# Queries, keys and values of two images as 64-row matmuls side by side, and values moved from unit 1 to unit 3

## The chip, the cores and the metric

The kernel runs on one core of a Trainium2 chip. The metric is the device time of that core in microseconds. Three runs of the kernel before gave 184.57, 183.47 and 184.43 us, a median of 184.43 us.

## The reference, cut to what matters

The input is 32 images of 64 channels by 16 x 16 pixels. A gate comes first, then group norm and attention with 4 heads of 16 channels over the 256 pixels of each image.

```
def _L0_conv_ref(x, w_c, w_s):               # channel gate, then spatial gate
    y = conv1d(mean(x, (2, 3)), w_c); yc = sigmoid(x * y)
    sa = sigmoid(conv2d(concat(mean(yc, 1), max(yc, 1)), w_s))
    return yc * sa + x

def _L1_conv_ref(x, gn_w, gn_b, qkv_w, qkv_b, proj_w, proj_b):
    xn = groupnorm(x, 32 groups) * gn_w + gn_b
    q, k, v = split(einsum('bchw,oc->bohw', xn, qkv_w) + qkv_b, 3)
    attn = softmax(einsum('bndi,bndj->bnij', q, k) / sqrt(16))
    out = einsum('bnij,bndj->bndi', attn, v)
    return x + einsum('bchw,oc->bohw', out, proj_w) + proj_b
```

## The kernel before

Two images make a pair: image 0 of a pair lies on partitions 0 to 63, image 1 on partitions 64 to 127, one channel each. There are 16 pairs. The attention is a software pipeline: `pipeline(eng, turn)` (L186) runs `turn(k)` on every engine for k = -5 to 17, and one turn holds eight units u = 0 to 7, one for each image and head. The order inside a turn is written out by hand, the same on each engine, and engines meet only at semaphores. In turn k, TensorE works on several pairs at once:

- `s(u)` (L761, matmuls L768) makes the scores of pair k+1 for unit u: two bf16 matmuls of 256 columns. VectorE takes their maximum over a row (L608). Two banks alternate, so `s(u)` waits for the maximum of unit u-2.
- `st(u)` (L772, matmuls L780) makes the transposed scores with the maximum subtracted by one extra row; ScalarE turns them into exponentials (L448).
- `maxt()` (L841, matmul L847) at unit 0 transposes the maxima of pair k. It waits for the last maximum of the turn before, and for `gn_var` of that turn, which VectorE writes after it (L561).
- `qk(a, d)` (L798, matmul L805) makes queries and keys of image a into its half of `z_bank`: all 128 partitions of `xn` against a weight matrix whose rows for the other image are zero. The call is float32, and the trace shows each float32 matmul as two MATMUL instructions. Image 0 of pair k+4 comes at unit 7 of turn k, image 1 of the same pair at unit 0 of the turn after. ScalarE reads the bank twice, at unit 0 (L456) and unit 1 (L459, `z32`), and GpSimd and SyncE split it into bf16 parts and spread them through DRAM.
- `v()` (L809, matmul L815) at unit 1 makes the values of both images of pair k+1, pixels by channels: per 128 pixels one float32 matmul with `xn` as weights and a block-diagonal 128 x 128 `w_v` as moving operand. ScalarE copies them to `vs` at unit 2 (L465).
- `pv(a)` (L784, matmul L794) at units 2 and 4 multiplies exponentials and values of pair k-1 in float32, with weights of 32 columns, four heads on four column groups. `proj()` (L818, matmul L824) at unit 4 does the output projection of pair k-2, also with weights of 32 columns.
- `groupstats(5)` (L828) at unit 6 serves the group norm of pair k+5, and GpSimd (L339 to L365) and ScalarE (L440, `xn`) finish it.
- VectorE also transposes and normalises the output of `pv`: L575, L579, L581, L586.

In PSUM, banks 0 to 3 belong to `s` and `st`, bank 4 to `pv`, bank 5 to `z_bank`, bank 6 to `v_psum`, `mt_psum` and `gs_psum`, bank 7 to `y_psum` of `proj`.

Of the kernel before, what the change touches and what calls it, by code (L numbers as in the profile page):

```python
# [38 lines left out]
MAPS = ((0, 1), (1, 2)) + tuple((p, p + 2) for p in range(2, PAIRS, 2))  # L39
EPS = 1e-5  # L40
LEAD = HEADS
SCALE = float(HD) ** -0.5
TWIN = (SIDE // TILES + KS - 1) * SIDE
HALO = KS // 2 * SIDE
# [10 lines left out]
def program(nc, x, vecs, w_all, select, consts, out):  # L55
    ctx = ExitStack()
    with ctx:
# [3 lines left out]
        def sem(name):  # L61
            return ctx.enter_context(nc.semaphore(name))

        quad = ctx.enter_context(nc.psum_tensor("quad", [P, 4, 512], F32))
        bank = [quad[:, i, :] for i in range(4)] + [ctx.enter_context(nc.psum_tensor(f"bank{i}", [P, 512], F32)) for i in range(4, 8)]
        parts_dram = nc.dram_tensor("parts_dram", [RING, 3, 2, HD, HEADS * 2 * N], BF16).ap()
        gate_dram = nc.dram_tensor("gate_dram", [IMAGES, N], F32).ap()

# [35 lines left out]
        negmax = sb("negmax", [P, RING, P], BF16)  # L104
        maxrow = sb("maxrow", [16, RING, P], BF16)
        pt = sb("pt", [P, UNITS, TILES, N])
        vs = sb("vs", [P, RING, TILES, 2, HEADS, 2 * HD])
        rstd = sb("rstd", [P, 1])
        mhalf = sb("mhalf", [P, 1])
        eps = sb("eps", [P, 1])  # L110
# [14 lines left out]
        st_bank = [bank[2], bank[3]]  # L125
        o_bank = bank[4]
        z_bank = bank[5]
        v_psum = bank[6][:, 0:256]
        mt_psum = bank[6][:, 320:384].bitcast(BF16)
        y_psum = bank[7][:, 0:256]  # L130
        gs_psum = bank[6][:, 400:403]


# [47 lines left out]
        def stands_in(aside, k, u):  # L181

            if isinstance(k, int) and (k, u) in aside:
                aside[k, u]()

        def pipeline(eng, turn):  # L186

# [121 lines left out]
        @block.gpsimd  # L309
        def _(pool):  # L310
            nc.gpsimd.memset(eps[:, :], EPS).then_inc(eps_ready, 1)
            nc.gpsimd.memset(mhalf[:, :], -0.5).then_inc(mhalf_ready, 1)
            nc.gpsimd.memset(warm[:, :], 0.0).then_inc(warm_ready, 1)
            nc.gpsimd.memset(negmax[:, :, :], 0.0).then_inc(negmax_zero, 1)
            pool.wait_ge(mhalf_ready, 1)
            pool.wait_ge(eps_ready, 1)

            nc.gpsimd.memset(vs[:, :, :, :, :, :].rearrange("p r t a h d -> p (r t a h) d")[:, :, HD:2 * HD], 1.0).then_inc(fixed_ready, 1)
            pool.wait_ge(fixed_ready, 1)
            nc.gpsimd.memset(ks[KQ:KQ + 1, :, :, :, :], 1.0).then_inc(fixed_ready, 1)  # L320
            pool.wait_ge(fixed_ready, 2)
            pool.wait_ge(vec_in, 16)

            def turn(k, slot, has, lap):

                if has(-3):
                    wait(pool, yo_ready, k - 2)
                    nc.gpsimd.tensor_tensor(at(xall, k - 3), yo[:, slot(-3), :], at(xall, k - 3), ALU.add).then_inc(out_ready, 1)  # L328

                if has(5) and not (isinstance(k, int) and k + 5 in EARLY):  # L330
                    if isinstance(k, int) and k + 4 in EARLY:
                        pool.wait_ge(x1_ready, k + 5)
                    for g in [(k + 5) // GROUP] if isinstance(k, int) else range(1, GROUPS):
                        pool.wait_ge(gate_in[g], 32)
                    nc.gpsimd.tensor_tensor(at(ycall, k + 5), at(ycall, k + 5), at(gate, k + 5), ALU.mult).then_inc(u_ready, 1)  # L335
                    pool.wait_ge(u_ready, k + 6)
                    nc.gpsimd.tensor_tensor(at(xall, k + 5), at(ycall, k + 5), at(xall, k + 5), ALU.add).then_inc(x1_ready, 1)

                if has(4):  # L339
                    wait(pool, gn_var, k + 5)  # L340
                    nc.gpsimd.tensor_tensor(sq[:, :], gmv[:, 2:3], gmv[:, 2:3], ALU.mult).then_inc(sq_ready, 1)  # L341
                    nc.gpsimd.tensor_tensor(posvar[:, :], eps[:, :], gmv[:, 1:2], ALU.subtract).then_inc(posvar_ready, 1)
                    wait(pool, sq_ready, k + 5)
                    wait(pool, posvar_ready, k + 5)
                    nc.gpsimd.tensor_tensor(vareps[:, :], sq[:, :], posvar[:, :], ALU.add).then_inc(vareps_ready, 1)
                    wait(pool, vareps_ready, k + 5)
                    nc.gpsimd.tensor_tensor(rstd[:, :], vareps[:, :], mhalf[:, :], ALU.pow).then_inc(rstd_ready, 1)

                on_pool = has(3) and not (isinstance(k, int) and k + 3 == 0)
                if on_pool:  # L350
                    r = slot(3)
                    wait(pool, p1_ready, k + 4)
                    wait(pool, z32_ready, k + 3)
                    wait(pool, split_step, 3 * (k + 3))
                    nc.gpsimd.tensor_tensor(rest[:, :], z32[:, :], parts[:, r, 0, :], ALU.subtract).then_inc(split_step, 1)  # L355
                    wait(pool, split_step, 3 * (k + 3) + 1)

                if has(4):
                    wait(pool, rstd_ready, k + 5)
                    wait(pool, xn_ready, k + 4)  # L360
                    nc.gpsimd.tensor_tensor(gna[:, :], rstd[:, :], w_gn, ALU.mult).then_inc(gn_scale, 1)
                    wait(pool, gn_scale, k + 5)
                    nc.gpsimd.tensor_tensor(gnm[:, :], gmv[:, 0:1], gna[:, :], ALU.mult).then_inc(gn_mean, 1)
                    wait(pool, gn_mean, k + 5)
                    nc.gpsimd.tensor_tensor(gnb[:, :], gnm[:, :], b_gn, ALU.add).then_inc(gn_shift, 1)  # L365
                if on_pool:
                    nc.gpsimd.tensor_scalar(parts[:, r, 1, :], rest[:, :], 1.0, 0.0, ALU.mult, ALU.add).then_inc(split_step, 1)
                    wait(pool, st_ready, UNITS * k)
                    wait(pool, split_step, 3 * (k + 3) + 2)
                    nc.gpsimd.tensor_tensor(parts[:, r, 2, :], rest[:, :], parts[:, r, 1, :], ALU.subtract).then_inc(split_step, 1)  # L370
            pipeline(pool, turn)
# [3 lines left out]
        def _(act):  # L375
# [54 lines left out]
            def turn(k, slot, has, lap):  # L430
                for u in range(UNITS):
# [19 lines left out]
                    if u == 0 and has(3):  # L451
                        wait(act, z_ready, k + 4)
                        wait(act, parts_out[0], 16 * (k - 1))
                        if isinstance(k, int) and k == 1:
                            act.wait_ge(stack_in[0], 2 * SLOTS * 16)
                        nc.scalar.activation(parts[:, slot(3), 0, :], z_bank[:, :], ACT.Identity, bias=b_qk).then_inc(p1_ready, 1)  # L456
                    if u == 1 and has(3) and not (isinstance(k, int) and k + 3 == 0):
                        wait(act, split_step, 3 * (k + 2) + 1)
                        nc.scalar.activation(z32[:, :], z_bank[:, :], ACT.Identity, bias=b_qk).then_inc(z32_ready, 1)  # L459

                    if u == 2 and has(1):
                        if isinstance(k, int) and k == -1:
                            act.wait_ge(pbias_ready, 1)
                        wait(act, v_ready, k + 2)
                        nc.scalar.copy(vs[:, slot(1), :, :, :, :].rearrange("p t a h d -> p (t a h) d")[:, :, 0:HD],  # L465
                                       v_psum.rearrange("p (g d) -> p g d", d=HD)).then_inc(vs_ready, 1)

                    if u == 5 and has(-2) and not (isinstance(k, int) and k - 2 == PAIRS - 1):
                        wait(act, y_ready, k - 1)
# [166 lines left out]
        def _(pe):  # L636
# [123 lines left out]
            def turn(k, slot, has, lap):  # L760
# [23 lines left out]
                def pv(a):  # L784
# [6 lines left out]
                        wait(pe, vs_ready, k)  # L791
                    for t in range(TILES):
                        for h in range(HEADS):
                            mm = pe.matmul(o_bank[32 * h:32 * h + 32, a * N:(a + 1) * N], vs[:, slot(-1), t, a, h, :],  # L794
                                           pt[:, HEADS * a + h, t, :], start=(t == 0), stop=(t == TILES - 1))
                    mm.then_inc(pv_done, 1)

                def qk(a, d):  # L798
# [7 lines left out]
                    if a == 1:  # L806
                        mm.then_inc(z_ready, 1)

                def v():  # L809

                    wait(pe, mrow_ready, k + 1)
                    if has(4):
                        wait(pe, gn_var, 4 if isinstance(k, int) and k == 0 else k + 5)
                    for t in range(TILES):
                        mm = pe.matmul(v_psum[:, t * P:(t + 1) * P], xn[:, slot(1), t * P:(t + 1) * P], w_v, start=True, stop=True)  # L815
                    mm.then_inc(v_ready, 1)

                def proj():  # L818

                    wait(pe, norm_step, 4 * PAIRS + 4 if isinstance(k, int) and k == PAIRS + 1 else 4 * (k - 1))  # L820
                    wait(pe, yo_ready, k - 2)
                    for a in range(2):
                        for j in range(0, C, 32):
                            mm = pe.matmul(y_psum[C * a + j:C * a + j + 32, :], w_p[:, j:j + 32], onorm[:, a * N:(a + 1) * N],  # L824
# [26 lines left out]
                for u in range(UNITS):  # L851
# [9 lines left out]
                    if u == 0 and has(0):  # L861
                        maxt()
                    if u == 0 and has(3) and not first_turns:
                        qk(1, 3)
                    if u == 1 and has(1):
                        v()
                    if u == 2 and has(-1):
                        pv(0)
                    if u == 4 and has(-2):
# [4 lines left out]
                        groupstats(5)  # L874
                    if u == 2 and isinstance(k, int) and k == 0:
                        groupstats(4)
                    if u == 7 and has(4) and not (first_turns and k < -1):
                        qk(0, 4)
                    if first_turns:
                        beginning(k, u, qk, groupstats)  # L880
# [59 lines left out]
```

## Time and profile before

| what | value |
|---|---|
| median of 3 runs | 184.43 us |
| profiled execution, its own time | 184.61 us |
| its span, first to last instruction | 182.6 us |
| mean granted TensorE clock | 0.947 |
| TensorE matmul busy | 163.2 us |
| VectorE busy | 136.5 us |
| ScalarE busy | 121.6 us |
| GpSimd busy | 106.3 us |

The busy time of TensorE counts overlapping matmuls once, and the ends of its matmuls are modelled; the start of one matmul to the start of the next is the firmer measure. Outside the span lie 2.0 us of the profiled execution's own time.

### The profile page before, as it was taken

The numbers are of one execution on the slowest core, as the hardware profiler recorded it, in microseconds if no ns is written. First come the engines' busy times: TensorE is split into PE (matmuls) and PEld (weight loads), VectorE is DVE, ScalarE is ACT, GpSimd is POOL, SyncE is SP. The second block draws the span as 40 slices with busy tenths as digits, with TensorE's granted clock in tenths as the row PEclk, the third lists the DMA queues.
The fourth block names the chain that finished last, engine by engine and source line by source line (L and its number), as shares of the span: only waits on it lengthen the run. The fifth ranks groups of instructions, "written<-read, shape, count | busy, mean of one in ns | idle before, by whom it ended". The sixth has DMA issues, their size and how long they took to land.

```text
span 182.6 us, 4762 instructions
## 1 busy us (share of the span) xinstructions
PE 163.2 (89%) x1508; PEld 107.3 (59%) x1511; DVE 136.5 (75%) x280; ACT 121.6 (67%) x254; POOL 106.3 (58%) x206
## 2 busy tenths in 40 slices
PE   6988829999685999999999999999999999998791
PEld 3778428776451857666675766767575754553220
DVE  1567663677661889898998989899897978876433
ACT  3552343455682679887987988798797965758730
POOL 8926072681977267888888778888858350101110
PEclk9999955899997899999999999999999999999967
DMA  5940487516189544555464564564646465110001
GB/s 138 336 149 0 100 105 224 153 59 176 63 196 232 151 134 130 173 164 187 130 204 148 162 201 148 169 183 163 173 132 186 139 203 148 36 32 30 29 0 57
DMA packets 19296, 25.31 MB, mean 139 GB/s; under 512 B 3568, under 2 KB 16400, under 8 KB 19280
## 3 DMA queue, kind: packets, MB, share of 16 engines
q1 hardware_dynamic: 18560, 24.62, 46.2%
q10 hardware_dynamic: 720, 0.48, 1.6%
q8 instruction: 9, 0.15, 0.4%
q14 instruction: 7, 0.06, 0.1%
HBM read 16.22 MB, written 8.02 MB: 133 GB/s over the span
## 4 chain that ended last, share of the span: by engine, by line
PE 77%; DVE 5%; ACT 4%; POOL 4%; issue 3%; DMA 2%; ACTq 2%; SPq 2%; POOLq 0%
PE bank L794 17%; PE quad L768 16%; PE quad L780 14%; PE bank L805 7%; PE bank L824 5%; PE quad L662 5%; PE bank L815 4%; PE bank L640 2%; DMA qs<-maxrow 2%; PE bank L674 2%; ACT pt L448 2%; ACTq L217 2%; DVE negmax L608 2%; PE bank L838 1%; POOL rest L355 1%
## 5 line engine op out<-in xcount | busy, mean ns | idle before, releaser
L608 DVE TENSOR_REDUCE negmax<-quad 128x2 bf16<-128x512 f32 x128 | 83.4, 678 | 21.1 <-PE quad L768 19.4
L448 ACT ACTIVATE pt<-quad 128x512 f32<-128x512 f32 x128 | 72.8, 594 | 23.2 <-PE quad L780 23.2
L780 PE MATMUL quad<-qs,ks 97*128 97x256 bf16 x256 | 49.4, 275 | 6.7 <-ACT pt L448 3.5
L768 PE MATMUL quad<-ks,qs 96*128 96x256 bf16 x256 | 50.5, 279 | 1.2 <-DVE negmax L608 0.4
L794 PE MATMUL bank<-pt,vs 128*32 128x256 f32 x512 | 35.8, 399 | 0.0
L768 PEld LDWEIGHTS quad<-ks,qs 96*128 96x128 bf16 x256 | 21.9, 101 | 22.3 <-DVE negmax L608 13.1
L780 PEld LDWEIGHTS quad<-qs,ks 97*128 97x128 bf16 x256 | 23.8, 98 | 14.7 <-ACT pt L448 6.3
L328 POOL TENSOR_TENSOR xall<-yo,xall 128x256 f32 (+1 forms) x15 | 11.0, 731 | 31.7 <-ACT yo L472 31.7
L794 PEld LDWEIGHTS bank<-pt,vs 128*32 128x32 f32 x512 | 15.1, 112 | 12.9 <-ACT pt L448 3.3
L355 POOL TENSOR_TENSOR rest<-z,parts 128x512 f32<-128x512 f32 x15 | 17.3, 1156 | 8.0 <-issue 5.9
L805 PE MATMUL bank<-xn,wall 128*128 128x256 f32 x64 | 19.9, 397 | 0.0
L370 POOL TENSOR_TENSOR parts<-rest,parts 128x512 bf16<-128x512 f32 x15 | 17.3, 1155 | 1.5
L456 ACT ACTIVATE parts<-bank,vec 128x512 bf16<-128x512 f32 x16 | 10.8, 675 | 10.4 <-PE bank L805 7.3
L575 DVE STREAM_TRANSPOSE otok<-bank 128x512 f32<-128x512 f32 (+1 forms) x17 | 11.5, 677 | 5.9 <-PE bank L794 5.9
L440 ACT ACTIVATE xn<-xall,gnb,gna 128x256 f32<-128x256 f32 (+1 forms) x16 | 9.6, 599 | 7.4 <-POOL gnb L365 7.2
L341 POOL TENSOR_TENSOR sq<-gmv 128x1 f32<-128x1 f32 x16 | 3.1, 194 | 17.5 <-DVE gmv L561 17.4
L586 DVE STREAM_TRANSPOSE onorm<-otok 128x512 f32<-128x512 f32 (+1 forms) x17 | 11.6, 680 | 1.2 <-PE bank L824 0.6
L824 PE MATMUL bank<-onorm,wall 128*32 128x256 f32 x128 | 10.7, 406 | 1.6 <-DVE onorm L586 1.6
L662 PE MATMUL quad<-con,ycall 128*128 128x130 f32 x64 | 10.8, 321 | 0.1
L805 PEld LDWEIGHTS bank<-xn,wall 128*128 128x128 f32 x64 | 10.0, 194 | 1.1 <-issue 0.6
L335 POOL TENSOR_TENSOR ycall<-ycall,gate (+1 forms) x12 | 8.7, 726 | 3.3 <-DMA gate<-gate_dram 3.3
L815 PE MATMUL bank<-wall,xn 128*128 128x128 f32 x64 | 10.4, 287 | 0.0
(66 smaller groups left out, 207.7 us busy)
## 6 DMA issues: line engine op xcount, KB each, us to landing
parts_dram<-parts SPq DMA_DIRECT2D x45, 128.0 KB, 2.0
ks<-parts_dram SPq DMA_DIRECT2D x15, 192.0 KB, 3.0
qs<-parts_dram SPq DMA_DIRECT2D x15, 192.0 KB, 3.2
out<-xall SPq DMA_DIRECT2D x16, 128.0 KB, 2.1
qs<-parts_dram SPq DMA_DIRECT2D x15, 128.0 KB, 2.7
ks<-parts_dram SPq DMA_DIRECT2D x15, 128.0 KB, 2.8
xall<-x SPq DMA_DIRECT2D x3, 512.0 KB, 6.0
gate<-gate_dram SPq DMA_DIRECT2D x6, 256.0 KB, 4.1
```

Source lines behind the costliest of these rows:

```text
L355: nc.gpsimd.tensor_tensor(rest[:, :], z32[:, :], parts[:, r, 0, :], ALU.subtract).then_inc(split_step, 1)
L370: nc.gpsimd.tensor_tensor(parts[:, r, 2, :], rest[:, :], parts[:, r, 1, :], ALU.subtract).then_inc(split_step, 1)
L448: nc.scalar.activation(pt[:, (u + LEAD) % UNITS, :, :].rearrange("p t n -> p (t n)"), st_bank[u % 2][:, :], ACT.Exp, scale=SCALE).then_inc ...
L586: op = nc.vector.transpose(onorm[:, cols], o_tok[:, blocks, :].rearrange("p b c -> p (b c)"))
L608: nc.vector.tensor_reduce(negmax[:, slot(1), column:column + TILES], s_bank[u % 2][:, :].rearrange("p (t n) -> p t n", t=TILES), AX.X, ALU ...
L662: mm = pe.matmul(bank[MAP_BANK[i] + p - first][:, t * (P + 2):(t + 1) * (P + 2)], ycall[:, p, t * P:(t + 1) * P], con[:, C_IDENT:C_TOEP], ...
L768: mm = pe.matmul(s_bank[u % 2][:, t * N:(t + 1) * N], qs[0:KQ, slot(1), h, a, t * P:(t + 1) * P], ks[0:KQ, slot(1), h, a, :], start=True, ...
L780: mm = pe.matmul(st_bank[u % 2][:, t * N:(t + 1) * N], ks[0:KQ + 1, slot(d), h, a, t * P:(t + 1) * P], qs[0:KQ + 1, slot(d), h, a, :], sta ...
L794: mm = pe.matmul(o_bank[32 * h:32 * h + 32, a * N:(a + 1) * N], vs[:, slot(-1), t, a, h, :], pt[:, HEADS * a + h, t, :], start=(t == 0), s ...
L805: mm = pe.matmul(z_bank[:, a * N:(a + 1) * N], w_qk[a], xn[:, slot(d), :], start=True, stop=True)
L815: mm = pe.matmul(v_psum[:, t * P:(t + 1) * P], xn[:, slot(1), t * P:(t + 1) * P], w_v, start=True, stop=True)
L824: mm = pe.matmul(y_psum[C * a + j:C * a + j + 32, :], w_p[:, j:j + 32], onorm[:, a * N:(a + 1) * N], start=True, stop=True)
```

## The change

Three things change. (1) From turn 1 on (`apart(k)`), `qk_apart` replaces the two calls of `qk`: at unit 0 it makes queries and keys of both images of pair k+3, each with the 64 rows of its own image as contraction, into different banks; nothing of it is left at unit 7. (2) From turn 1 on, `v_apart` replaces `v`: four float32 matmuls of 64 rows by 128 weight columns and 64 moving columns, image 0 to one bank and image 1 to another, at unit 3 in place of unit 1; ScalarE's copy goes from unit 2 to unit 3. (3) PSUM is laid out as one tensor of eight banks so that `z_halves` and `v_halves` straddle two neighbouring banks; `y_psum` moves to the bank of `z`, `vs` has image before tile, and waits are added for what now shares a bank.

```diff
+FIRST_APART = 1
-        quad = ctx.enter_context(nc.psum_tensor("quad", [P, 4, 512], F32))
-        bank = [quad[:, i, :] for i in range(4)] + [ctx.enter_context(nc.psum_tensor(f"bank{i}", [P, 512], F32)) for i in range(4, 8)]
+        quad = ctx.enter_context(nc.psum_tensor("quad", [P, 8, 512], F32))
+        bank = [quad[:, i, :] for i in (0, 1, 2, 3, 4, 5, 7, 6)]
-        vs = sb("vs", [P, RING, TILES, 2, HEADS, 2 * HD])
+        vs = sb("vs", [P, RING, 2, TILES, HEADS, 2 * HD])
+        z_halves = quad[:, 5:7, :].rearrange("p b (h n) -> p (b h) n", n=N)[:, 1:3, :]
+        v_halves = quad[:, 6:8, :].rearrange("p b n -> p (b n)")[:, 384:640]
-        y_psum = bank[7][:, 0:256]
+        y_psum = bank[5][:, 0:256]
+        def apart(k):
+            return not isinstance(k, int) or k >= FIRST_APART
...
-                        nc.scalar.activation(parts[:, slot(3), 0, :], z_bank[:, :], ACT.Identity, bias=b_qk).then_inc(p1_ready, 1)
+                        nc.scalar.activation(per_image(parts[:, slot(3), 0, :]), queries_of(k), ACT.Identity, bias=b_qk).then_inc(p1_ready, 1)
...
-                    if u == 2 and has(1):
+                    if u == (3 if apart(k) else 2) and has(1):
...
+                def qk_apart():
+
+                    wait(pe, xn_ready, k + 4)
+                    wait(pe, z32_ready, k + 2)
+                    wait(pe, yo_ready, k - 2)
+                    for a in range(2):
+                        mm = pe.matmul(z_halves[:, a, :], w_qk[a][C * a:C * (a + 1), :], xn[C * a:C * (a + 1), slot(3), :], start=True, stop=True)
+                    mm.then_inc(z_ready, 1)
...
+                def v_apart():
+
+                    wait(pe, mrow_ready, k + 1)
+                    if has(4):
+                        wait(pe, gn_var, k + 5)
+                    if has(3):
+                        wait(pe, z32_ready, k + 3)
+                    for t in range(TILES):
+                        for a in range(2):
+                            at_ = (a * TILES + t) * C
+                            mm = pe.matmul(v_halves[:, at_:at_ + C], xn[C * a:C * (a + 1), slot(1), t * P:(t + 1) * P],
+                                           w_v[C * a:C * (a + 1), C * a:C * (a + 1)], start=True, stop=True)
+                    mm.then_inc(v_ready, 1)
...
                     wait(pe, yo_ready, k - 2)
+                    if has(3):
+                        wait(pe, z32_ready, k + 3)
...
                     if u == 0 and has(3) and not first_turns:
-                        qk(1, 3)
-                    if u == 1 and has(1):
+                        if apart(k):
+                            qk_apart()
+                        else:
+                            qk(1, 3)
+                    if u == 1 and has(1) and not apart(k):
                         v()
+                    if u == 3 and has(1) and apart(k):
+                        v_apart()
...
-                    if u == 7 and has(4) and not (first_turns and k < -1):
+                    if u == 7 and has(4) and not apart(k + 1) and not (first_turns and k < -1):
                         qk(0, 4)
```

## Rows read from the trace of the kernel before

**Rows 1.** Chain that ended last: start us, us, what; 11 repeats from first to last.
```profile
61.77 0.43 PE bank L805 x2
...
141.28 0.43 PE bank L805 x2
```

**Rows 2.** Busy time by stretch: window, length, busy us (instructions) of each engine, clock.
```profile
core 0: us, PE busy (x) PEld busy (x) DVE busy (x) ACT busy (x) POOL busy (x), PEclk, DMA share, GB/s
88.36:96.32 7.96, 7.96 (x90) 5.49 (x91) 7.38 (x16) 6.79 (x16) 6.63 (x14) 1.00 0.56 169
```

**Rows 3.** Timeline of TensorE matmuls in one turn: start us, us, what.
```profile
89.55 0.38 PE L780 MATMUL quad<-qs,ks 97*128 97x256 bf16 x2
...
90.00 0.38 PE L780 MATMUL quad<-qs,ks 97*128 97x256 bf16 x2
90.31 0.64 PE L824 MATMUL bank<-onorm,wall 128*32 128x256 f32 x8
90.76 1.05 PE L794 MATMUL bank<-pt,vs 128*32 128x256 f32 x16
91.74 0.39 PE L768 MATMUL quad<-ks,qs 96*128 96x256 bf16 x2
...
93.44 0.59 PE L805 MATMUL bank<-xn,wall 128*128 128x256 f32 x2
93.87 0.38 PE L768 MATMUL quad<-ks,qs 96*128 96x256 bf16 x2
94.09 0.38 PE L780 MATMUL quad<-qs,ks 97*128 97x256 bf16 x2
94.32 0.22 PE L847 MATMUL bank<-identb,negmax 128*128 128x128 bf16 x1
94.38 0.65 PE L805 MATMUL bank<-xn,wall 128*128 128x256 f32 x2
94.86 0.38 PE L768 MATMUL quad<-ks,qs 96*128 96x256 bf16 x2
...
95.30 0.61 PE L815 MATMUL bank<-wall,xn 128*128 128x128 f32 x4
95.75 0.38 PE L768 MATMUL quad<-ks,qs 96*128 96x256 bf16 x2
```

**Rows 4.** Timeline of VectorE, same turn; in brackets the idle time before.
```profile
92.17 1.93 DVE L608 TENSOR_REDUCE negmax<-quad 128x2 bf16<-128x512 f32 x3 [0.39 <-PE quad L768]
...
94.02 0.15 DVE L561 TENSOR_SCALAR gmv<-bank 128x3 f32<-128x3 f32 x1
```

**Rows 5.** Timeline of weight loads (PEld), same turn.
```profile
94.29 0.10 PEld L847 LDWEIGHTS bank<-identb,negmax 128*128 128x128 bf16 x1
...
95.20 0.52 PEld L815 LDWEIGHTS bank<-wall,xn 128*128 128x128 f32 x4
```

**Rows 6.** Timeline around the only matmuls with few rows (4).
```profile
20.16 1.13 PE L695 MATMUL quad<-gate_s,sel 4*128 4x256 f32 x4
21.22 0.70 PE L805 MATMUL bank<-xn,wall 128*128 128x256 f32 x2
```

**Rows 7.** Those matmuls by line: durations min/median/max ns, first and last start.
```profile
L695 PE MATMUL quad<-gate_s,sel x4: 374/374/478, 20.2 to 20.9; 4*128 4x256 f32 x4
```

**Rows 8.** Timeline of the first 0.08 us of a 16-matmul group.
```profile
88.32 0.42 PE L794 MATMUL bank<-pt,vs 128*32 128x256 f32 x4
```

**Rows 9.** Timeline of ScalarE in the same turn.
```profile
88.31 0.69 ACT L459 ACTIVATE z<-bank,vec 128x512 f32<-128x512 f32 x1
...
92.89 0.47 ACT L472 ACTIVATE yo<-bank,pbias 128x256 f32<-128x256 f32 x1
```

**Rows 10.** Timeline of TensorE in turns 1 and 13, with idle time before.
```profile
57.01 0.38 PE L780 MATMUL quad<-qs,ks 97*128 97x256 bf16 x2 [3.04 <-DMA qs<-maxrow]
...
153.74 0.38 PE L780 MATMUL quad<-qs,ks 97*128 97x256 bf16 x2 [0.42 <-ACT pt L448]
```

More of the change, by code:

```diff
@@ L184, in stands_in, with queries_of, per_image @@
                 aside[k, u]()
+        def apart(k):
+            return not isinstance(k, int) or k >= FIRST_APART
+        def queries_of(k):
+            return z_halves if apart(k) else per_image(z_bank[:, :])
+        def per_image(t):
+            return t.rearrange("p (a n) -> p a n", a=2)
         def pipeline(eng, turn):
@@ L316, in _ @@
             pool.wait_ge(eps_ready, 1)
-            nc.gpsimd.memset(vs[:, :, :, :, :, :].rearrange("p r t a h d -> p (r t a h) d")[:, :, HD:2 * HD], 1.0).then_inc(fixed_ready, 1)
+            nc.gpsimd.memset(vs[:, :, :, :, :, :].rearrange("p r a t h d -> p (r a t h) d")[:, :, HD:2 * HD], 1.0).then_inc(fixed_ready, 1)
             pool.wait_ge(fixed_ready, 1)
@@ L455, in turn @@
                             act.wait_ge(stack_in[0], 2 * SLOTS * 16)
-                        nc.scalar.activation(parts[:, slot(3), 0, :], z_bank[:, :], ACT.Identity, bias=b_qk).then_inc(p1_ready, 1)
+                        nc.scalar.activation(per_image(parts[:, slot(3), 0, :]), queries_of(k), ACT.Identity, bias=b_qk).then_inc(p1_ready, 1)
                     if u == 1 and has(3) and not (isinstance(k, int) and k + 3 == 0):
                         wait(act, split_step, 3 * (k + 2) + 1)
-                        nc.scalar.activation(z32[:, :], z_bank[:, :], ACT.Identity, bias=b_qk).then_inc(z32_ready, 1)
-                    if u == 2 and has(1):
+                        nc.scalar.activation(per_image(z32[:, :]), queries_of(k), ACT.Identity, bias=b_qk).then_inc(z32_ready, 1)
+                    if u == (3 if apart(k) else 2) and has(1):
                         if isinstance(k, int) and k == -1:
@@ L464, in turn @@
                         wait(act, v_ready, k + 2)
-                        nc.scalar.copy(vs[:, slot(1), :, :, :, :].rearrange("p t a h d -> p (t a h) d")[:, :, 0:HD],
-                                       v_psum.rearrange("p (g d) -> p g d", d=HD)).then_inc(vs_ready, 1)
+                        nc.scalar.copy(vs[:, slot(1), :, :, :, :].rearrange("p a t h d -> p (a t h) d")[:, :, 0:HD],
+                                       (v_halves if apart(k) else v_psum).rearrange("p (g d) -> p g d", d=HD)).then_inc(vs_ready, 1)
                     if u == 5 and has(-2) and not (isinstance(k, int) and k - 2 == PAIRS - 1):
@@ L793, in pv @@
                         for h in range(HEADS):
-                            mm = pe.matmul(o_bank[32 * h:32 * h + 32, a * N:(a + 1) * N], vs[:, slot(-1), t, a, h, :],
+                            mm = pe.matmul(o_bank[32 * h:32 * h + 32, a * N:(a + 1) * N], vs[:, slot(-1), a, t, h, :],
                                            pt[:, HEADS * a + h, t, :], start=(t == 0), stop=(t == TILES - 1))
@@ L814, in v @@
                     for t in range(TILES):
-                        mm = pe.matmul(v_psum[:, t * P:(t + 1) * P], xn[:, slot(1), t * P:(t + 1) * P], w_v, start=True, stop=True)
+                        mm = pe.matmul(v_psum.rearrange("p (a t n) -> p a t n", a=2, t=TILES)[:, :, t, :], xn[:, slot(1), t * P:(t + 1) * P], w_v,
+                                       start=True, stop=True)
+                    mm.then_inc(v_ready, 1)
[10 more added lines that the diff above has]
+                                           w_v[C * a:C * (a + 1), C * a:C * (a + 1)], start=True, stop=True)
                     mm.then_inc(v_ready, 1)
```

## The prediction

> **What bounds the kernel now.** I read the chain that ended last first. Between 60 and 142 us it runs almost only through TensorE, and its pieces repeat: the matmuls of `qk` for image 0 stand in it eleven times, from 61.77 to 141.28 us [rows 1]. That is 79.51 us for ten turns, a period of 7.95 us. Then I read the busy time of one such turn: TensorE 7.96 of 7.96 us, at the full clock (1.00, the 2.4 GHz level), VectorE 7.38 us, ScalarE 6.79 and GpSimd 6.63 [rows 2]. TensorE paces these turns, but VectorE is close behind. VectorE waits for scores once in a turn, 0.39 us before the maximum of unit 5 [rows 4], so a turn can't get shorter than 7.95 - 0.39 = 7.56 us whatever TensorE saves.
>
> Third, the timeline of a turn shows who waits for whom. `s(5)` starts at 91.74; the maximum of unit 5 starts 0.43 us later, three maxima take until 94.10, and `gmv` ends at 94.02 + 0.15 = 94.17 [rows 3, 4]. `maxt` waits for `gmv`, and its weight load starts at 94.29 [rows 5], 0.12 us later. Some 0.04 us of that goes to the semaphore (the maximum starts 0.04 us after the end of the matmul at 91.74 + 0.39), so 0.08 us is left. So there is a loop through both engines: `s(5)`, three maxima, `gmv`, `maxt`, and then all of TensorE's work down to the next `s(5)`. It takes 7.95 - 0.08 = 7.87 us now. It is this loop that decides: work taken from TensorE between `s(5)` and `maxt` saves 0.08 us at most, work added behind `maxt` counts in full.
>
> **Removed.** From start to start of the next matmul, `qk` of image 0 at unit 7 takes 93.87 - 93.44 = 0.43 us, `qk` of image 1 94.86 - 94.38 = 0.48 us, `v` 95.75 - 95.30 = 0.45 us [rows 3]. The first lies before `maxt`: of its 0.43 us the loop gets 0.08.
>
> **Price of changing the shape of the array.** The change puts 64-row matmuls between 128-row ones. The trace has no 64-row matmul, but has two kinds of neighbours. The first are `proj` and `pv`, of 32 weight columns. Into `proj`: the second matmul of `st(4)` starts 0.11 us (half of the 0.22 between rows) after 90.00 and takes 0.11, so it is through at 90.22, and `proj` starts at 90.31, 0.09 us late. Out of `pv(1)`: its 16 matmuls start at 90.76; at four column groups side by side they need 4 x 0.213 = 0.853 us (0.213 is half of `qk`'s 0.43); `s(5)` starts at 91.74, 0.13 us late [rows 3]. The second neighbour is the gate's pair of matmuls with 4 rows and 128 weight columns. Their first lasts 478 ns against 374 for the others, so 0.10 us of weight load is laid bare, and after the last start, 20.9 + 0.21 us, the next 128-row matmul starts 0.11 us late [rows 6, 7]. I take 0.09 + 0.10 in and 0.13 out, 0.32 us each visit, since the new weights too have 128 float32 columns. Bounds: nothing (it never shows) and 0.42 us, with another 0.10 us for a bare load on the way out, as 0.70 us for two `qk` matmuls there against 0.59 in the steady turn suggests [rows 3, 6].
>
> The Trainium skill speaks here (TensorEngine Tiling (Array Packing), Key Properties): changing the tiling mode, not merely the tile, drains the engine. By that rule the 64-row case is no exception to the rows just read; no run here shows that case yet.
>
> **Added at unit 0: `qk_apart`.** Two float32 matmuls of 256 columns on two halves of the rows, four instructions. If the halves run side by side, 2 x 0.213 = 0.43 us. That column groups do so shows in the four `pv` matmuls that start within 0.08 us [rows 8]; for row groups no row shows it, so the bounds are 0.43 and 0.85 us. I take 0.43, since the nearest row is a concurrent one. With the visit: 0.43 + 0.32 = 0.75 us. What it replaces behind `maxt` is 0.48 us plus nothing else. The difference is +0.27; a little of the load is already bare after `maxt` (0.48 against 0.43) and is counted in both.
>
> **Added at unit 3: `v_apart`.** Half the moving columns, but eight weight loads of 128 columns where there were four. The four loads of `v` take 0.52 us and one 0.19, so they come every (0.52 - 0.19)/3 = 0.11 us [rows 5], and `v` is already paced by loads as much as by columns. With the halves side by side: four loads, 0.10 (in the visit's price) + 3 x 0.11 + 0.05 for the last 64 columns = 0.38 us and the 0.32, 0.70 us. If the loads of the halves follow each other, four more: +0.43, 1.13 us. If only columns counted, 4 x 0.053 = 0.21. I take 0.70, by concurrency as above. Against 0.45 removed, +0.25 us. Its move from unit 1 to unit 3 keeps it in the same stretch between `maxt` and `s(5)`, so the move neither helps nor hurts the loop.
>
> By the same page's Theoretical Speedup, 64 rows give up to twofold. By that alone `qk_apart` would cost 0.43 and `v_apart` 0.22 us, and the loop would fall to VectorE's floor; that result is the first rival below.
>
> **Edits at nothing.** `v_apart` waits for `z32`, with `s(4)`, `st(4)`, `proj`, `pv(1)` queued behind it. `z32` is ready at 88.31 + 0.69 = 89.00 [rows 9], `st(3)` is through at 89.77 [rows 3]: 0.77 us of cover; without it each late bit would count in full. `proj`'s wait for `z32` has 1.3 us. `qk_apart` waits for `yo`, done at 93.36, 1 us before [rows 9]. ScalarE's copy of the values comes about 1.2 us later; the first who wait are `groupstats` at unit 6 and then `maxt`, both over a microsecond away. The ScalarE instructions that read two banks have the same elements (bound: 0.1 us each if they were slower, covered by 1.2 us of ScalarE's idle time). SyncE's and GpSimd's orders don't change; their input `z` comes at 94.24 + 0.05 + 0.19 + 0.43 and the same latency, within 0.1 us of now. Turn 1 waits 3.04 us for a DMA behind `v`'s new place [rows 10], so its edits are hidden. In turn 13 `st(4)` waits 0.42 us for ScalarE [rows 10], which covers the move of `v` there; turn 14 may add 0.25.
>
> **Sum.** The loop: 7.87 + 0.27 + 0.25 = 8.39 us, +0.44 us a turn. TensorE's own total is lower, 7.95 - 1.36 + 1.45 = 8.04 us, so it would idle some 0.35 us a turn before `maxt`. From `s(5)` of turn 1 to that of turn 12 are eleven turns: 11 x 0.44 = +4.8 us. Against the profiled execution's own 184.61 us that is 189.4 us; this execution lies 0.18 us above the median, so 189.2, and I say 189.0, a little of the visit's price being perhaps shared with the gap already behind `maxt`.
>
> **Rivals.**
> (a) *Visits cost nothing and loads hide, faster.* Next weights are fetched while the last 128-row matmuls run, and the halves overlap. The price from which it decides: below 0.06 us a visit (2 x 0.32 less 0.52) the loop is no longer than 7.87, and faster than now by over 1% needs also `v`'s loads to shrink. With `v_apart` at 0.21 and `qk_apart` at 0.43 the loop is 7.87 - 0.05 - 0.24 = 7.58 us, at VectorE's floor of 7.56: 11 x -0.37 = -4.1, 180.4 us. With loads at their pace, 7.87 - 0.05 - 0.02 = 7.80: -1.7, 182.8 us. For it: the halves touch different rows. Against it: the 4-row pair paid on both sides [rows 6, 7]. Chance 0.15.
> (b) *About half the visit's price*, because some of it is latency that the next row's start hides: 8.39 - 0.32 = 8.07, +0.12 a turn, 185.8 us. TensorE's own total then lies beneath the loop. Chance 0.15.
> (c) *Halves overlap as matmuls, but their weight loads come one after another*: +0.43 more in `v_apart`, loop 8.82, +0.87 x 11 = 9.6, 194.0 us. Chance 0.12.
> (d) *Row halves don't run side by side at all, the change does not do what it says*: +0.43 in `qk_apart` as well, loop 9.25, +14.3, 198.7 us. Chance 0.07.
>
> **How the numbers follow.** The forecast has 0.51. A measurement of this kernel tells about 1% (1.8 us) from no change. Faster by over 1%, below 182.6: 0.12, most of (a). Within 1%: 0.16, the rest of (a) and most of (b), whose 185.8 lies just inside. Slower: 0.72. The range leaves out what of (a) lies below its upper value (0.11) and (d) (0.07), with the least of the edges: 182.7 to 194.2. The forecast's own range is 187 to 191.
>
> **What would show it.** In a steady turn of the changed kernel: from the start of `qk_apart`'s first matmul to the next `s` about 0.6 to 0.7 us, with a gap ahead of it; from `v_apart`'s first start to `s(4)` about 0.6; the four instructions of `qk_apart` starting in twos shows the overlap, one by one shows (d). Eight loads of `v_apart` in about 0.5 us against 0.9 tells the forecast from (c). TensorE idle before `maxt`, ended by `gmv`, shows the loop, and VectorE's idle time before unit 5 should grow from 0.39 to about 0.8. A period under 7.95 us would make the prediction wrong, and so would 64-row matmuls whose loads start before the last 128-row matmul has ended.

## The result and the profile after

The changed kernel is slower. Six runs have a median of 192.56 us (189.46 to 193.26), against 184.12 us (182.69 to 185.91) for the kernel before; the ratio is 1.035, with a 95% interval of 1.028 to 1.043. The ratios and intervals, here and in the table below, compare only executions outside a slower state that both kernels fall into at times, so they aren't the quotients of the medians: of the changed kernel two of the six remain (190.30 and 189.46 us), and where the table says none, too few remain. The forecast of 189.0 us was 1.025 times the median then shown. The profiled execution took 192.36 us, its span is 190.4 us.

The chain that ended last in the changed kernel, where the 16 matmuls of `pv(1)` mark a turn (start us, us, what; turns 2, 12 and 15):

```profile
68.88 0.86 PE quad L806 x16
...
153.60 0.86 PE quad L806 x16
...
176.81 0.97 PE quad L806 x16
```

And the same three marks in the kernel before:

```profile
67.08 0.86 PE bank L794 x16
...
146.57 0.86 PE bank L794 x16
...
168.96 0.97 PE bank L794 x16
```

The 7.8 us between the two spans (190.4 - 182.6) divide so: 68.88 - 67.08 = 1.8 us up to turn 2; ten turns of 8.47 instead of 7.95 us, 84.72 - 79.49 = 5.2 us; three turns after them 23.21 instead of 22.39 us, 0.8 us; and the rest, 13.59 against 13.64, nothing. Half of the first piece comes before turn 1 (ScalarE's `maxrow` copy of turn 1 starts at 51.32 against 50.43 us), where the two kernels do the same work but for the layout of PSUM. It doesn't come with the change: the changed kernel profiled once more was at that copy at 49.37 us, and its whole span was 188.5 us. Of the other half, 0.40 us lies between that copy and `st(4)` of turn 1, which waits for the DMA of the maxima (6.98 us against 6.58; 6.79 in the second profile), so that part isn't shown to be the change's either. The remaining 0.51 us are the two visits of turn 2 to 64 rows. The change thus accounts for 0.5 + 5.2 + 0.8 = 6.5 us, which is 3.5% of 184 us.

One turn of the changed kernel, the timeline of TensorE (start us, us, what; it answers to [rows 3]):

```profile
92.24 0.38 PE L792 MATMUL quad<-qs,ks 97*128 97x256 bf16 x2
92.55 0.66 PE L850 MATMUL quad<-wall,xn 64*128 64x64 f32 x8
93.14 0.39 PE L780 MATMUL quad<-ks,qs 96*128 96x256 bf16 x2
...
93.69 0.64 PE L862 MATMUL quad<-onorm,wall 128*32 128x256 f32 x8
94.14 1.05 PE L806 MATMUL quad<-pt,vs 128*32 128x256 f32 x16
95.12 0.39 PE L780 MATMUL quad<-ks,qs 96*128 96x256 bf16 x2
...
97.27 0.39 PE L792 MATMUL quad<-qs,ks 97*128 97x256 bf16 x2
97.70 0.22 PE L885 MATMUL quad<-identb,negmax 128*128 128x128 bf16 x1
97.98 0.70 PE L827 MATMUL quad<-xn,wall 64*128 64x256 f32 x4
98.61 0.39 PE L780 MATMUL quad<-ks,qs 96*128 96x256 bf16 x2
```

`qk_apart` takes 98.61 - 97.98 = 0.63 us and `v_apart` 93.14 - 92.55 = 0.59 us from start to start, each with a gap ahead of it: `v_apart` starts 92.55 - 92.24 = 0.31 us after `st(3)`, where 0.22 is usual. `qk_apart` starts 0.28 us after `maxt` here and 0.14 in most turns, against 0.06 before (94.38 - 94.32 in [rows 3]). In the median over the steady turns these four distances add up to 0.14 + 0.64 + 0.31 + 0.59 = 1.68 us, and what they replace to 0.06 + 0.48 + 0.22 + 0.45 = 1.21 us. That is 0.47 of the 0.50 us by which a turn grew; all other distances between `maxt` and `s(5)` are those of before to 0.01 us, so the new layout of PSUM and the added waits cost nothing there. The weight loads of the same turn, with the idle time before them and what ended it:

```profile
92.55 0.52 PEld L850 LDWEIGHTS quad<-wall,xn 64*128 64x128 f32 x8 [0.21 <-issue]
...
97.67 0.10 PEld L885 LDWEIGHTS quad<-identb,negmax 128*128 128x128 bf16 x1 [0.29 <-DVE negmax L620]
97.95 0.33 PEld L827 LDWEIGHTS quad<-xn,wall 64*128 64x128 f32 x4 [0.18 <-issue]
98.61 0.11 PEld L780 LDWEIGHTS quad<-ks,qs 96*128 96x128 bf16 x2 [0.33 <-issue]
```

Eight loads of `v_apart` take 0.52 us, as four of `v` did [rows 5]: the two row halves load side by side. No load stands ahead of a change of shape; each begins within 0.03 us of its matmul, where `v`'s loads began 0.10 us ahead (95.20 against 95.30 in [rows 3, 5]). `maxt`'s load now waits idle for VectorE. VectorE in that turn (it answers to [rows 4]):

```profile
95.55 1.93 DVE L620 TENSOR_REDUCE negmax<-quad 128x2 bf16<-128x512 f32 x3 [0.82 <-PE quad L780]
97.40 0.15 DVE L573 TENSOR_SCALAR gmv<-quad 128x3 f32<-128x3 f32 x1
```

Its wait for the scores of unit 5 grew from 0.39 to 0.82 us, and the three maxima and `gmv` follow `s(5)` at the same distances as before. Busy times of one such turn (it answers to [rows 2]):

```profile
81.00:89.46 8.46, 8.43 (x92) 5.03 (x91) 7.33 (x16) 6.95 (x14) 6.63 (x14) 1.00 0.52 154
```

TensorE's busy time reads 8.43 of 8.46 us though it waits at `maxt` and at each change of shape: the modelled ends of its matmuls cover these gaps, and only starts show them. The granted clock is at its full level (1.00) in both kernels' steady turns. It isn't so around turn 1: there TensorE waits about 3 us for the DMA of the maxima (3.04 us before, 2.93 after), and right behind that wait the clock reads 0.50, the 1.2 GHz level, before the change in the window of 58 to 60 us, after it in that of 60 to 62 us.

### The profile page after: what moved, and what is told of

Read it like the earlier page. It is cut to its first block, busy times and chain, and to the rows that moved or that the text cites. A ratio compares the mean times of both kernels' runs of the same rounds, so it can differ in the third digit from the quotient of the medians.

```text
span 190.4 us, 4883 instructions
## 1 busy us (share of the span) xinstructions
PE 170.0 (89%) x1567; PEld 102.5 (54%) x1567; DVE 136.2 (72%) x280; ACT 123.9 (65%) x254; POOL 106.3 (56%) x206
## 3 DMA queue, kind: packets, MB, share of 16 engines
HBM read 16.22 MB, written 8.02 MB: 127 GB/s over the span
## 4 chain that ended last, share of the span: by engine, by line
PE 75%; DVE 8%; issue 4%; ACT 4%; POOL 4%; DMA 2%; ACTq 2%; SPq 1%; POOLq 0%
PE quad L780 16%; PE quad L806 16%; PE quad L792 13%; PE quad L862 5%; PE quad L674 5%; PE quad L850 4%; PE quad L827 4%; DVE negmax L620 3%; PE quad L652 3%; DMA qs<-maxrow 2%; PE quad L686 2%; ACTq L229 2%; PE quad L876 1%; PE quad L817 1%; ACT pt L460 1%
## 5 line engine op out<-in xcount | busy, mean ns | idle before, releaser
L460 ACT ACTIVATE pt<-quad 128x512 f32<-128x512 f32 x128 | 74.0, 596 | 28.8 <-PE quad L792 28.8
L806 PE MATMUL quad<-pt,vs 128*32 128x256 f32 x512 | 35.5, 397 | 0.0
L780 PEld LDWEIGHTS quad<-ks,qs 96*128 96x128 bf16 x256 | 18.9, 101 | 27.2 <-DVE negmax L620 15.9
L806 PEld LDWEIGHTS quad<-pt,vs 128*32 128x32 f32 x512 | 15.1, 112 | 12.7 <-issue 3.8
L468 ACT ACTIVATE parts<-quad,vec 128x512 bf16<-128x512 f32 x16 | 11.0, 685 | 11.7 <-PE quad L817 7.5
L587 DVE STREAM_TRANSPOSE otok<-quad 128x512 f32<-128x512 f32 (+1 forms) x17 | 11.5, 677 | 5.9 <-PE quad L806 5.9
L862 PE MATMUL quad<-onorm,wall 128*32 128x256 f32 x128 | 10.7, 406 | 1.6 <-DVE onorm L598 1.6
L471 ACT ACTIVATE z<-quad,vec 128x512 f32<-128x512 f32 x15 | 10.3, 687 | 0.0
L674 PEld LDWEIGHTS quad<-con,ycall 128*128 128x128 f32 x64 | 9.6, 226 | 0.8 <-issue 0.4
L652 PE MATMUL quad<-warm 128*128 128x512 bf16 x19 | 8.5, 494 | 1.4 <-POOL warm L325 1.4
```

Of the source, the lines that this page charges most:

```text
L460: nc.scalar.activation(pt[:, (u + LEAD) % UNITS, :, :].rearrange("p t n -> p (t n)"), st_bank[u % 2][:, :], ACT.Exp, scale=SCALE).then_inc ...
L587: op = nc.vector.transpose(o_tok[:, blocks, :].rearrange("p b c -> p (b c)"), o_bank[:, cols])
L652: pe.matmul(bank[:, :], warm[:, 0:P], warm[:, :], start=True, stop=True)
L674: mm = pe.matmul(bank[MAP_BANK[i] + p - first][:, t * (P + 2):(t + 1) * (P + 2)], ycall[:, p, t * P:(t + 1) * P], con[:, C_IDENT:C_TOEP], ...
L780: mm = pe.matmul(s_bank[u % 2][:, t * N:(t + 1) * N], qs[0:KQ, slot(1), h, a, t * P:(t + 1) * P], ks[0:KQ, slot(1), h, a, :], start=True, ...
```

## The experiments

The totals of these kernels spread by some microseconds from run to run, and the profiles show much of it ahead of the steady turns: ScalarE's `maxrow` copy of turn 3 starts anywhere from 70.3 to 76.6 us, at 72.44 and at 70.32 us in two profiles of the changed kernel. So the steady turn is read from each trace: the distance between the starts of ScalarE's `maxrow` copies, once a turn, the median and the mean of the eight turns from turn 3 to turn 11.

| kernel | median turn | mean turn | ratio to before (95%) |
|---|---|---|---|
| before | 7.96 | 7.96 | 1 |
| changed | 8.46 | 8.51 | 1.035 (1.028 to 1.043) |
| values only | 8.34 | 8.35 | 1.011 (0.994 to 1.029) |
| queries and keys only | 8.21 | 8.25 | none |
| values only moved, 128 rows | 8.10 | 8.17 | 1.006 (0.997 to 1.015) |
| queries and keys at unit 7 | 7.94 | 7.99 | 1.012 (0.999 to 1.026) |
| before with a 64-row visit | 8.38 | 8.38 | none |
| before with its 128-row twin | 8.09 | 8.11 | 1.002 (0.995 to 1.008) |
| changed, image 0 only | 8.45 | 8.48 | 1.035 (1.022 to 1.049) |
| changed, filler before maxt | 8.46 | 8.48 | 1.035 (1.022 to 1.048) |
| unit 7, maxima in another bank | 7.98 | 8.02 | 1.002 (0.997 to 1.007) |
| changed, again | 8.47 | 8.50 | 1.022 (1.009 to 1.035) |
| unit 7, maxima in another bank, maxt first | 7.93 | 7.96 | 0.987 (0.981 to 0.994) |

In the changed kernel three of the eight turns have 0.14 to 0.21 us more between `maxt` and `qk_apart`, in its second profile the same three; the turn shown above is one of them. They lift the mean over the median, in all kernels with `qk_apart` behind `maxt`. The kernel before has none of these, and I haven't found what delays them. In the other kernels single turns are longer by other waits, up to 8.57 us in the one with the values moved.

**Values only.** The changed kernel with queries and keys left as they were:

```diff
-                        if apart(k):
-                            qk_apart()
-                        else:
-                            qk(1, 3)
+                        qk(1, 3)
...
-                    if u == 7 and has(4) and not apart(k + 1) and not (first_turns and k < -1):
+                    if u == 7 and has(4) and not (first_turns and k < -1):
+                        wait(pe, yo_ready, k - 1)
                         qk(0, 4)
```

> Only the values are made by 64-row matmuls at unit 3; queries and keys stay as two 128-row matmuls at units 7 and 0. Loop theory (everything between maxt and s(5) counts in full, a visit to 64-row mode costs about 0.32 us): v costs 0.70 instead of 0.45 us, a steady turn goes from 7.95 to 8.20 us, with three drain turns at the end about 0.3 to 1.5 us more, so 3 to 4.3 us slower in all. Rival, the two changes only hurt together (the wait on z32 or the shared banks): within 1 us of the kernel before.

The turn is 8.34 us, 0.14 us more than expected; its median is 189.04 us (186.11 to 190.31). The added wait is needed because `y_psum` now shares the bank of `z`.

**Queries and keys only.** The values stay at unit 1 with 128 rows:

```diff
-                    if u == (3 if apart(k) else 2) and has(1):
+                    if u == 2 and has(1):
...
-                    if u == 1 and has(1) and not apart(k):
+                    if u == 1 and has(1):
                         v()
-                    if u == 3 and has(1) and apart(k):
-                        v_apart()
```

> Only queries and keys are made by 64-row matmuls at unit 0; values stay at unit 1 as 128-row matmuls. Loop theory: nothing gained at unit 7, since TensorE then waits for gmv, and +0.27 us behind maxt: a steady turn of 8.22 us, 3 us slower over 11 turns. Rival, TensorE's own total decides: 7.95 - 0.91 + 0.75 = 7.79 us a turn, 1.8 us faster.

8.21 us: the loop, not TensorE's total, which would give 7.79. The 0.43 us taken away at unit 7 bought nothing. The median of its four runs is 190.06 us (184.02 to 192.9), too wide to say more. In the profiled one turn 2 took 10.54 us, with the granted clock at 0.50 from 62 to 70 us; its steady turns are at the full level.

**Values moved, nothing else.** The kernel before with 128-row `v` at unit 3:

```diff
-                    if u == 1 and has(1):
+                    if u == (1 if isinstance(k, int) and k < 1 else 3) and has(1):
                         v()
```

(ScalarE's copy likewise.)

> The 128-row v and its copy by ScalarE move from unit 1 to unit 3, nothing else. Loop theory: v stays between maxt and s(5), steady turn 7.95 us as before; at the end, where TensorE has slack at unit 1 but not at unit 3, up to 1 us. Rival, the move is what costs: steady turn of 8.2 us or more, 3 us slower.

8.10 us, between the two theories: the move alone costs 0.14 us. TensorE's timeline and, in the second fence, its weight loads show two waits, in turns of that kernel:

```profile
91.97 0.39 PE L780 MATMUL quad<-qs,ks 97*128 97x256 bf16 x2 [0.31 <-DMA qs<-maxrow]
```

```profile
88.84 0.11 PEld L768 LDWEIGHTS quad<-ks,qs 96*128 96x128 bf16 x2 [0.24 <-DVE negmax L608]
```

At unit 1 `v` filled the time in which `s(2)` would wait for the maximum of unit 0; moved away, it lays that wait bare, and `s(2)` starts 0.34 us after `st(1)` in place of 0.22. That is nearly all of the 0.14 us. The wait of `st(4)` for the DMA with the maxima comes in two turns only. In the first experiment the same wait of `s(2)` costs just 0.06 us; the other 0.08 of its 0.14 us stand at unit 7, where `qk(0)` takes 0.51 us in place of 0.43 and its loads start 0.02 us ahead of it, not 0.11. It has the added wait there; whether that wait does it was not tried. What the 64-row shape costs the values is read from the starts: 0.09 us more ahead of `v_apart` and 0.14 more in it, 0.23 us. The difference of the two kernels, 8.34 - 8.10 = 0.24 us, agrees only because their other waits happen to be equally long. In the changed kernel `qk_apart` comes late enough that `s(2)` doesn't wait, and the parts add up: 0.25 for queries and keys (8.21 - 7.96) and 0.25 more to 8.46.

**Queries and keys at unit 7, ahead of `maxt`.**

```diff
-                    wait(pe, xn_ready, k + 4)
-                    wait(pe, z32_ready, k + 2)
-                    wait(pe, yo_ready, k - 2)
+                    wait(pe, xn_ready, k + 5)
+                    wait(pe, z32_ready, k + 3)
+                    wait(pe, yo_ready, k - 1)
...
-                    if u == 7 and has(4) and not apart(k + 1) and not (first_turns and k < -1):
-                        qk(0, 4)
+                    if u == 7 and has(4) and not (first_turns and k < -1):
+                        if apart(k + 1):
+                            qk_apart()
+                        else:
+                            qk(0, 4)
```

The values are those of the kernel before, at unit 1.

> Queries and keys by 64-row matmuls, but at unit 7 of the turn before, ahead of maxt; values as before at unit 1. Loop theory: behind maxt 0.48 us of work is gone, the loop falls to 7.47 us and no longer decides; TensorE's own total does: 7.95 - 0.91 + 0.75 = 7.79 us a turn, 11 x -0.16 = 1.8 us faster. Rival, 64-row matmuls cost more than they save wherever they stand: slower by 1 us or more.

7.94 us: the same 64-row matmuls cost 0.27 us a turn less than behind `maxt` (8.21), so the place decides, but the gain over the kernel before didn't come. The weight loads of `v` show a wait that is new:

```profile
91.10 0.52 PEld L836 LDWEIGHTS quad<-wall,xn 128*128 128x128 f32 x4 [0.18 <-ACT maxrow L448]
```

With nothing between `maxt` and `s(1)`, `v` comes so soon that it waits for ScalarE's copy out of the bank that both use. It starts 0.07 us late and takes 0.55 us in place of 0.45, in all 0.17 us, about what was missing (7.94 - 7.79). A later kernel takes this wait away.

**A visit to 64-row mode, by itself.** The kernel before with one tiny matmul ahead of those of `s(4)`; the twin has 128 in place of 64:

```diff
+                    if u == 4 and not (isinstance(k, int) and k < 1):
+                        pe.matmul(s_bank[0][:, 0:8], xn[0:64, slot(1), 0:P], w_v[0:64, 0:8], start=True, stop=True)
```

> The kernel before, with one tiny float32 matmul (64 rows, 128 weight columns, 8 moving columns) ahead of the matmuls of s(4) in every turn from 1 on, into columns that s(4) overwrites. Visit theory: 0.09 in, 0.10 bare load, 0.11 second load, 0.13 out, so from the end of st(3) to the start of s(4) about 0.43 us, and 0.4 us more a turn, 4.5 us in all. Rival, no price for the shape: as its 128-row twin.

> The twin of the 64-row visit: the same tiny matmul with all 128 rows. Both theories: its weights are fetched behind earlier matmuls, so it costs its two loads at most, 0.21 us a turn, about 2.3 us in all. The difference to the 64-row twin is the price of the shape: visit theory 0.2 to 0.25 us a turn, 2.5 us in all; rival 0.

8.38 against 8.09 us: the shape alone costs 0.29 us a turn, somewhat above the 0.20 to 0.25 expected, and the whole visit 0.42, as expected. The medians of the two are 189.62 us (187.3 to 191.92) and 185.44 us (182.51 to 190.11), with the kernel before at 183.80 beside them. TensorE's timeline of the 64-row kernel, then of its twin:

```profile
89.98 0.38 PE L782 MATMUL quad<-qs,ks 97*128 97x256 bf16 x2
90.30 0.39 PE L768 MATMUL quad<-wall,xn 64*128 64x8 f32 x2
90.61 0.39 PE L770 MATMUL quad<-ks,qs 96*128 96x256 bf16 x2
```

```profile
91.68 0.38 PE L782 MATMUL quad<-qs,ks 97*128 97x256 bf16 x2
91.90 0.28 PE L768 MATMUL quad<-wall,xn 128*128 128x8 f32 x2
92.04 0.38 PE L770 MATMUL quad<-ks,qs 96*128 96x256 bf16 x2
```

Between `st(3)` and `s(4)` it is 90.61 - 89.98 = 0.63 us against 0.36. Less its second load of 0.10 us, the visit of 0.42 us comes to 0.32, the price that went into the forecast for 64 and 256 columns: a matmul of eight columns pays as much for the shape.

**Image 0 only.** Half of the 64-row matmuls of the changed kernel are left out, so this kernel computes no queries, keys and values of image 1 from turn 1 on:

```diff
-                    for a in range(2):
+                    for a in range(1):
...
-                        for a in range(2):
+                        for a in range(1):
                             at_ = (a * TILES + t) * C
```

> The changed kernel without image 1: qk_apart and v_apart make only image 0, so half of their matmuls are left out (the results of image 1 are not computed). If the two row halves run side by side, this is as slow as the changed kernel, within 0.05 us a turn. If they run one after another, 0.43 us a turn less for queries and keys and 0.1 to 0.4 for values: 6 us less in all.

8.45 us against 8.46. TensorE's timeline of this kernel and, in the second fence, the weight loads of `v_apart`:

```profile
92.05 0.66 PE L850 MATMUL quad<-wall,xn 64*128 64x64 f32 x4
92.64 0.39 PE L780 MATMUL quad<-ks,qs 96*128 96x256 bf16 x2
...
97.34 0.70 PE L827 MATMUL quad<-xn,wall 64*128 64x256 f32 x2
97.97 0.39 PE L780 MATMUL quad<-ks,qs 96*128 96x256 bf16 x2
```

```profile
92.05 0.52 PEld L850 LDWEIGHTS quad<-wall,xn 64*128 64x128 f32 x4 [0.21 <-issue]
```

0.59 and 0.63 us, to the last digit those of both images together, and four loads take the 0.52 us of eight. The second half of the rows is free, loads included.

**A filler before `maxt`.** The changed kernel, with work that nobody needs:

```diff
+                    if u == 7 and not (isinstance(k, int) and k < 1):
+                        for _ in range(2):
+                            pe.matmul(st_bank[1][:, :], warm[:, 0:P], warm[:, :], start=True, stop=True)
```

> The changed kernel with two idle bf16 matmuls of 512 columns (0.43 us) ahead of st(7) in every turn from 1 on, in front of maxt. Loop theory: they fall into TensorE's wait for gmv and cost 0 to 0.1 us a turn, under 1.2 us in all. Rival, TensorE's total decides: 0.43 us a turn, 4.7 us more.

8.46 us with 0.43 us more work in each turn, not 8.89. The idle time ahead of `maxt` swallows it; this is the loop shown directly.

**Unit 7, with the maxima in another bank.**

```diff
-        mt_psum = bank[6][:, 320:384].bitcast(BF16)
+        mt_psum = bank[7][:, 320:384].bitcast(BF16)
...
+                    wait(pe, mrow_ready, k + 1)
...
-                    wait(pe, mrow_ready, k + 1)
+                    if not apart(k):
+                        wait(pe, mrow_ready, k + 1)
```

The first wait is added to `qk_apart`, the second is the one of `v`.

> The variant with queries and keys as 64-row matmuls at unit 7, and now the transposed maxima move to the other bank, so that v has no bank in common with ScalarE's copy of them and need not wait for it. In the variant without this, v started 0.07 us after st(1) was through and bared 0.10 us of weight load behind that wait. Wait theory: that 0.15 us a turn goes, the steady turn falls from 7.94 to 7.79 us (7.95 - 0.91 + 0.75), 1.8 us below the kernel before over 11 turns. Rival, something else fills the turn: 7.94 us and no gain.

The wait of `v` went, the time didn't: 7.98 us. So that wait was not what held the turn. The weight loads show the time again ahead of `st(4)`, which starts at 91.85, 0.34 us after `s(4)` at 91.51, where 0.22 us would do; `qk_apart` also starts 0.08 us later behind `st(7)` than in the first kernel with queries and keys at unit 7 (0.39 us against 0.31). The load of `st(4)`:

```profile
91.84 0.11 PEld L792 LDWEIGHTS quad<-qs,ks 97*128 97x128 bf16 x2 [0.23 <-issue]
```

**The changed kernel again.**

> The changed kernel once more, unedited, on the same chip as the others of this call: a steady turn of 8.46 us against 7.95, and 6 to 8 us more in all.

8.47 us a turn; 190.44 us (187.39 to 194.84) against 185.77, below the 6 to 8 us expected, with an interval that overlaps the first one. The size of the whole effect is known to a percent or so, that of a turn far better.

**`maxt` first.** On top of the unit-7 kernel with the other bank:

```diff
+                    if u == 0 and has(0) and apart(k):
+                        maxt()
                     if has(1):
...
-                    if has(4):
+                    if has(4) and not apart(k):
                         wait(pe, gn_var, 4 if isinstance(k, int) and k == 0 else k + 5)
                     mm = pe.transpose(mt_psum, negmax[:, slot(0), :], identb[:, :])
...
-                    if u == 5 and has(-2) and not (isinstance(k, int) and k - 2 == PAIRS - 1):
+                    if u == (4 if apart(k) and has(3) else 5) and has(-2) and not (isinstance(k, int) and k - 2 == PAIRS - 1):
```

> On top of the variant with queries and keys at unit 7 and the maxima in another bank, whose steady turn is 7.97 us: maxt now stands ahead of s(0) and no longer waits for gmv, and ScalarE makes yo right after the exponential of unit 4. Theory of a third loop (maxt, ScalarE's copy, the DMA qs<-maxrow of 2.7 us, st(4)): st(4) waited 0.12 us for that DMA and qk_apart 0.08 us for yo; both waits go, TensorE's own total of 7.79 us a turn is left, and over 11 turns 1.8 us less than the kernel before, about 1 percent. Rival, the turn has one more limit on ScalarE (the exponential of unit 2 ahead of st(4)): 7.95 us or more, no gain.

It is the one kernel of the set that measured faster than the kernel before, 0.987 (0.981 to 0.994), a difference under 2%; medians 184.61 us (181.54 to 190.87) and 186.16. The size of that is not explained: its shortest turns are 7.89 us, 0.07 below 7.96, which over 11 turns is 0.8 us and not 2.3, and the mean turn is no shorter at all. The kernel before had a median of 186.16 us beside it and of 184.12 us in the first comparison, so much of the gain may be that. The expected 7.79 didn't come. The DMA still ends a wait ahead of `st(4)`, but a short one (`st(4)` starts 0.25 us after `s(4)`, 0.03 more than usual). Most of the missing 0.14 us stands behind `maxt`, in the second fence:

```profile
91.92 0.11 PEld L792 LDWEIGHTS quad<-qs,ks 97*128 97x128 bf16 x2 [0.15 <-DMA qs<-maxrow]
```

```profile
96.10 0.23 PE L887 MATMUL quad<-identb,negmax 128*128 128x128 bf16 x1
96.30 0.38 PE L780 MATMUL quad<-ks,qs 96*128 96x256 bf16 x2
```

`maxt` is now the first matmul behind the 64-row ones, and `s(0)` starts 0.20 us after it; in the kernel with `maxt` behind `st(0)` the next matmul came 0.06 us after it. That is 0.14 us in most turns. `qk_apart` itself takes its usual 0.63 us (to the start of `maxt`, at 96.10). Why the matmul behind the small `maxt` comes so much later in this place was not tried.

## Why the prediction was right, step by step

The measured 192.56 us lies within the stated range of 182.7 to 194.2 us, but outside the 187 to 191 us that the prediction gave to its own forecast. The mechanism held, and the size came out too small: 6.5 us from the change against 4.8.

**The loop** was right and is shown. It predicted that work behind `maxt` counts and work ahead of it doesn't. Behind it, 64-row queries and keys made a turn of 8.21 us, ahead of it 7.94; a filler of 0.43 us ahead of it cost nothing; VectorE's wait for unit 5 grew to 0.82 us where about 0.8 was forecast.

**The slack of 0.08 us** ahead of `maxt` was not there. In the changed kernel, with TensorE idle, `gmv` ends at 97.55 us and the load of `maxt` starts at 97.67: 0.12 us, just what the kernel before had. I had counted 0.04 us for the semaphore from another pair of engines. The loop was 7.95 us long from the start, level with TensorE's own total, and the removed 0.43 us at unit 7 bought nothing, where I had 0.08. The 0.04 us was read from the modelled end of a matmul, and nothing in the rows said that it holds from VectorE to TensorE.

**The price of the shape** of 0.32 us held: `qk_apart` came out at +0.25 us (forecast +0.27) and `v_apart` at +0.24 (forecast +0.25), and the visit by itself at 0.42 us with its second load (0.43). The 8-column matmul shows that it doesn't depend on the number of columns. One of its readings was coarse: the 0.11 us behind the gate's matmuls came from a start given to 0.1 us, and the finer timeline gives 0.09; the 0.13 us taken for the way out was read elsewhere. The rule of the Trainium skill that a change of mode drains the engine (TensorEngine Tiling (Array Packing), Key Properties) agrees with these numbers, 64 rows included.

**Row halves side by side** held: leaving out one image changed neither 0.63 nor 0.59 us. Rivals (c) and (d) fall. The twofold gain that the Trainium skill names as the limit (TensorEngine Tiling (Array Packing), Theoretical Speedup) was there in the columns and the loads; the visit cost more than it returned. Rivals (a) and (b) fall with the 8.46 us turn.

**Sizes that were off.** A turn came to 8.46 us by its median, and 8.47 over the ten turns of the chain, where the sum said 8.39: 0.08 for the slack. That is 5.2 us in ten turns against 4.4; between turns 1 and 2 another 0.9 us went, where one turn's 0.44 stood in the sum: 0.51 us for the visits of turn 2 and 0.40 us ahead of `st(4)` in turn 1, which isn't shown to be the change's. At the end the forecast had at most 0.25 us, and the chain shows 0.8 us more between `pv(1)` of turn 12 and of turn 15. By the same marks the kernel with only the values made apart took 23.20 us there, that with only the 128-row `v` moved 22.70, against 22.39 before: 0.3 us for the move and 0.5 for the shape. There `v` at unit 1 stood partly in time that TensorE spent waiting, and at unit 3 it doesn't. The prediction's sentence that the move neither helps nor hurts failed there, and for the 128-row `v` also in the steady turn. The last 0.9 us of the profiled difference came before turn 1 and doesn't come with the change; with the 0.40 us it accounts for part of the distance between 189.0 and 192.56.

## What to carry to other kernels

When two engines pace a kernel almost equally, find the loop that goes through both before adding up either's work: taking work from one side of its wait buys nothing, adding on the other side costs all of it. Matmuls on half the rows are free for the second half, but the pair has to save more than one change of shape in and one out; what these runs suggest, though none of them tried it, is to gather such work into one visit that is long enough, next to other idle time. A step that is moved leaves a hole: see which wait it had been covering. And a wait taken away need not shorten anything: in the last kernels the time reappeared at the next wait, and what holds them at 7.9 to 8.0 us, where TensorE's sum says 7.79, is only in part explained.

## What the runs showed of the hardware

A float32 matmul of 64 rows, 128 weight columns and only 8 moving columns, between 128-row matmuls, cost 0.29 us more a turn than the same with 128 rows. Two row halves ran so well side by side that one or two images took the same time to 0.01 us, loads of 128 float32 columns included (eight in 0.52 us, one row half's four in 0.52 us too). And 0.12 us passed from the end of VectorE's `gmv` to TensorE's dependent weight load, where 0.04 us passed from the modelled end of a matmul to VectorE's start.
